# Thirteen layer norms of a transformer stack: column sums by matmul on features-on-partitions against row statistics with tokens turned onto partitions

## The reference

```python
def _layernorm(x, axis=-1, eps=1e-05):
    m = jnp.mean(x, axis=axis, keepdims=True)
    v = jnp.var(x, axis=axis, keepdims=True)
    return (x - m) / jnp.sqrt(v + eps)
...
x = x + _L0_xattn_ref(_layernorm(x), ctx_1024, ctx_1024, ...)
x = x + _L0_ffn_ref(_layernorm(x), ...)          # router, 8 experts of 512
...                                              # layers 1 and 2 alike
x = x + _L3_xattn_ref(_layernorm(x), ctx_1024, ctx_1024, ...)
x = x + _L3_ffn_ref(_layernorm(x), ...)          # router, 9 experts of 256
```

## Time and profile before

| | |
|---|---|
| median of 3 runs | 4042.69 us (4041.46 to 4049.66) |
| the profiled execution | 4052.49 us, its span 4050.8 us |
| PE busy | 3442.2 us, 85% of the span |
| DVE busy | 2414.1 us, 60% |
| ACT busy | 1848.2 us, 46% |
| POOL busy | 1175.3 us, 29% |
| the 13 norms, from first product to last result | 246.89 us, 6.1% of the span |

### The profile page before, as it was taken

The page is one execution under the profiler, slowest core; times in us unless marked ns, Lnnn a source line. Parts: engine busy times, 40 slices in busy tenths (PEclk is TensorE's granted clock), DMA queues, the critical chain, the costliest instruction groups (busy, mean ns, idle before and its releaser), DMA issues. The chain is left out here.

```text
span 4050.8 us, 78638 instructions
## 1 busy us (share of the span) xinstructions
PE 3442.2 (85%) x30966; PEld 2422.0 (60%) x30966; DVE 2414.1 (60%) x4465; ACT 1848.2 (46%) x3390; POOL 1175.3 (29%) x727
## 2 busy tenths in 40 slices
PE   6977986999999999999987998699999973348859
PEld 4643545887778787878865776355555542225534
DVE  2435544776666666767753443688888845646535
ACT  1423323555555555555542543266666631115526
POOL 0002541111111111111112111377777730025507
PEclk6988997999999999999998998699999975569879
DMA  3540002001001000010002664333333300044400
GB/s 72 123 92 33 1 2 67 32 32 47 32 32 45 35 32 32 32 45 35 29 10 89 236 238 174 79 96 85 89 94 83 93 2 6 0 76 92 77 25 10
DMA packets 155773, 253.60 MB, mean 63 GB/s; under 512 B 11301, under 2 KB 114994, under 8 KB 155154
## 3 DMA queue, kind: packets, MB, share of 16 engines
q1 hardware_dynamic: 155410, 248.49, 21.8%
HBM read 173.82 MB, written 74.65 MB: 61 GB/s over the span
## 5 line engine op out<-in xcount | busy, mean ns | idle before, releaser
L1679 DVE TENSOR_SCALAR_CACHE_REDUCE L_p<-L_score,L_cols 128x1500 f32<-128x1500 f32 x224 | 398.7, 1780 | 396.3 <-PE L_score L1515 396.3
L1618 ACT CAST L_pthi<-L_pt 125x512 bf16<-125x512 f32 x672 | 350.5, 593 | 557.1 <-PE L_pt L1524 557.1
L1961 ACT ACTIVATE L2b_p<-L2b_score 125x448 f32<-125x448 f32 x768 | 392.2, 542 | 300.3 <-PE L2b_score L1876 293.9
L1535 PE MATMUL L_acc<-L_chi,L_pthi 125*128 125x128 bf16 x2688 | 462.0, 219 | 0.4 <-DVE L_attn L1699 0.4
L1537 PE MATMUL L_acc<-L_chi,L_ptlo 125*128 125x128 bf16 x2688 | 461.6, 219 | 0.0
L1536 PE MATMUL L_acc<-L_clo,L_pthi 125*128 125x128 bf16 x2688 | 461.5, 219 | 0.0
L1692 DVE TENSOR_TENSOR L_ptlo<-L_pt,L_pthi 125x512 bf16<-125x512 f32 x672 | 418.2, 678 | 1.1 <-ACT L_pthi L1618 1.1
L1602 ACT ACTIVATE L_p<-L_p,L_least 128x1500 f32<-128x1500 f32 x224 | 350.3, 1564 | 7.2 <-DVE L_p L1679 5.2
L1524 PEld LDWEIGHTS L_pt<-ident,L_p 128*125 128x125 f32 x2688 | 332.1, 190 | 33.4 <-issue 1.3
L1524 PE MATMUL L_pt<-ident,L_p 128*125 128x128 f32 x2688 | 333.8, 274 | 0.5 <-ACT L_p L1602 0.4
L2032 DVE TENSOR_REDUCE L2b_max<-L2b_m 112x1 f32<-112x1000 f32 x256 | 301.9, 1193 | 42.0 <-PE L2b_m L1857 41.9
(11 more groups left out here) (595 smaller groups left out, 7219.9 us busy)
## 6 DMA issues: line engine op xcount, KB each, us to landing
L2b_kst<-L_keys SPq DMA_DIRECT2D x96, 375.0 KB, 5.5
L_ctx<-dram_ctx SPq DMA_DIRECT2D x32, 750.0 KB
L_ct<-L_ct SPq DMA_DIRECT2D x32, 750.0 KB
L2a_ct<-L_ct SPq DMA_DIRECT2D x32, 750.0 KB, 14.5
L_keys<-L2a_kout SPq DMA_DIRECT2D x32, 750.0 KB, 7.6
L_values<-L2a_vout SPq DMA_DIRECT2D x32, 750.0 KB
L2b_vin<-L_values SPq DMA_DIRECT2D x32, 750.0 KB
L0x_ctx<-dram_ctx SPq DMA_DIRECT2D x32, 672.0 KB
```

The source lines that it names most:

```text
L1535: pe.matmul(acc, pt_hi[k % 2][:, t, :], c_hi[half][:, t, :], start=(t == 0), stop=False)
L1618: act.copy(pt_hi[k % 2][:, 4 * j:4 * j + 4, :], pt_ps[j][0:KP, :].rearrange("p (t q) -> p t q", t=4)).then_inc(hi_done, 1)
L1679: dve.tensor_scalar(probs[k % 2][:, :].rearrange("p (i n) -> p i n", i=3), score_ps[:, :].rearrange("p (i n) -> p i n", i=3)[:, :, 0:500], ...
L1961: act.activation(probs[t % RP][:, half * 2 * GW:(half + 1) * 2 * GW], score_ps[half][0:KP, 0:2 * GW], ACT.Exp).then_inc(exp_done, 1)
```

## The change

`layernorm` is rewritten for all its calls, and layer 3's L3x_ln and L3x_lnq become one call (`twice`), so there are 12. PE turns the 14 groups of 128 tokens so that tokens stand on partitions (L211). DVE takes the statistics of each group from PSUM with one instruction (L252, it gives count, mean and sum of squares of even and odd elements), and makes variances of five small instructions (L261 to L268), first for groups 0 to 7, then for 8 to 13. POOL's power is in two parts accordingly (L242). ACT scales groups 0 to 7 with a scale and an offset per partition (L226), DVE groups 8 to 13 (L299). PE turns each group back (L217), and ACT copies the first 1024 columns out of PSUM (L234, or L236 with the weight and bias), DVE the rest (L279, or L277). Where the result is added to x, DVE takes all four chunks (L275) and has added the bias to x before (L293). All 8 PSUM banks are used, so that no engine waits for a bank.

```diff
-        layernorm(nc, c, "L3x_ln", c["xT"], c["hT"], 1e-5)
-        layernorm(nc, c, "L3x_lnq", c["hT"], c["hT"], 1e-5, col["w1"][:, :], col["b1"][:, :])
+        layernorm(nc, c, "L3x_lnq", c["xT"], c["hT"], 1e-5, col["w1"][:, :], col["b1"][:, :], twice=True)
...
+    floor = eps * eps / (1.0 + eps) if twice else eps / 4.0 if double else eps
+    grow = 1.0 + eps if twice else 1.0
+    groups = [(0, 4), (4, 4), (8, 4), (12, 2)]
+    halves = [(0, 8), (8, TT)]
...
+            def _(pe):
+                for g, (t0, n) in enumerate(groups):
+                    for t in range(n):
+                        m = pe.transpose(x_ps[g][:, t * 128:(t + 1) * 128], src[:, (t0 + t) * 128:(t0 + t + 1) * 128],
+                                         c["ident"][:, :])
+                    m.then_inc(turned, 1)
+                for g, (t0, n) in enumerate(groups):
+                    pe.wait_ge(first_rows if g < 2 else last_rows, 2 * k + g % 2 + 1)
+                    for t in range(n):
+                        m = pe.transpose(y_ps[g][:, t * 128:(t + 1) * 128], rows[:, t0 + t, :], c["ident"][:, :])
+                    m.then_inc(back_done, 1)
...
+            def _(act):
+                act.wait_ge(offset_ready, 2 * k + 1)
+                for g in (0, 1):
+                    t0, n = groups[g]
+                    for t in range(n):
+                        m = act.activation(rows[:, t0 + t, :], x_ps[g][:, t * 128:(t + 1) * 128], ACT.Identity,
+                                           bias=offset[:, t0 + t:t0 + t + 1], scale=rstd[:, t0 + t:t0 + t + 1])
+                    m.then_inc(first_rows, 1)
+                if add_to is None:
+                    for g in (0, 1):
+                        s, n = cols(g)
+                        act.wait_ge(back_done, 4 * k + g + 1)
+                        if gamma is None:
+                            act.copy(dst[:, s], y_ps[g][:, 0:n])
+                        else:
+                            act.activation(dst[:, s], y_ps[g][:, 0:n], ACT.Identity, bias=beta, scale=gamma)
...
+            def _(pool):
+                for h, (a, b) in enumerate(halves):
+                    pool.wait_ge(var_ready, 2 * k + h + 1)
+                    pool.tensor_tensor(rstd[:, a:b], var[:, a:b], c["half_neg"][:, a:b], ALU.pow).then_inc(rstd_ready, 1)
...
+                def statistics(h):
+                    a, b = halves[h]
+                    for g in (2 * h, 2 * h + 1):
+                        t0, n = groups[g]
+                        dve.wait_ge(turned, 4 * k + g + 1)
+                        for t in range(n):
+                            m = dve.bn_stats(stats[:, t0 + t, :], x_ps[g][:, t * 128:(t + 1) * 128])
+                    m.then_inc(stats_done, 1)
...
+                statistics(0)
+                variance(0)
+                statistics(1)
+                a, b = halves[0]
+                dve.wait_ge(rstd_ready, 2 * k + 1)
+                dve.scalar_tensor_tensor(offset[:, a:b], total[:, a:b], -0.5, rstd[:, a:b], ALU.mult, ALU.mult
+                                         ).then_inc(offset_ready, 1)
+                variance(1)
+                a, b = halves[1]
+                dve.wait_ge(var_ready, 2 * k + 2)
+                dve.tensor_scalar(offset[:, a:b], total[:, a:b], 0.5, None, ALU.mult).then_inc(offset_ready, 1)
+                if add_to is not None:
+                    dve.tensor_scalar(add_to[:, :], add_to[:, :], beta, None, ALU.add).then_inc(added, 1)
...
+                for g in (2, 3):
+                    t0, n = groups[g]
+                    for t in range(n):
+                        m = dve.tensor_scalar(rows[:, t0 + t, :], x_ps[g][:, t * 128:(t + 1) * 128],
+                                              offset[:, t0 + t:t0 + t + 1], rstd[:, t0 + t:t0 + t + 1], ALU.subtract,
+                                              ALU.mult)
+                    m.then_inc(last_rows, 1)
```

More of the change, by code:

```diff
@@ L245, in _ @@
[L245 to L259, removed]
@@ L260, in _ @@
-                for i in range(4):
-                    s, n = cols(i)
-                    dve.wait_ge(r_done, 4 * k + i + 1)
-                    ins = dve.tensor_tensor(dst[:, s], dst[:, s], r_ps[i % 2][:, 0:n], ALU.mult)
-                    ins.then_inc(scaled, 1)
-                    if gamma is not None or add_to is not None:
-                        dve.wait_ge(scaled, 4 * k + i + 1)
-                    if gamma is not None:
-                        st.link(dve.tensor_scalar(dst[:, s], dst[:, s], gamma, beta, ALU.mult, ALU.add))
-                    if add_to is not None:
-                        st.link(dve.tensor_tensor(add_to[:, s], add_to[:, s], dst[:, s], ALU.add))
@@ L271, in _, with variance, part @@
-                c["ln_count"]["steps"] += st.n
+                def statistics(h):
[6 more added lines that the diff above has]
+                    m.then_inc(stats_done, 1)
+                def variance(h):
+                    a, b = halves[h]
+                    def part(i):
+                        return stats[:, a:b, i:i + 1].rearrange("p t o -> p (t o)")
+                    dve.wait_ge(stats_done, 2 * k + h + 1)
+                    dve.tensor_tensor(gap[:, a:b], part(1), part(4), ALU.subtract).then_inc(parts_done, 1)
+                    dve.scalar_tensor_tensor(spread[:, a:b], part(2), D * floor, part(5), ALU.add, ALU.add)
+                    dve.wait_ge(parts_done, 4 * k + 2 * h + 1)
+                    dve.scalar_tensor_tensor(gap[:, a:b], gap[:, a:b], grow / 4.0, gap[:, a:b], ALU.mult, ALU.mult
+                                             ).then_inc(parts_done, 1)
+                    dve.tensor_tensor(total[:, a:b], part(1), part(4), ALU.add)
+                    dve.wait_ge(parts_done, 4 * k + 2 * h + 2)
+                    dve.scalar_tensor_tensor(var[:, a:b], spread[:, a:b], grow / D, gap[:, a:b], ALU.mult, ALU.add
+                                             ).then_inc(var_ready, 1)
@@ new lines, in evacuate @@
+                def evacuate(g):
+                    s, n = cols(g)
+                    dve.wait_ge(back_done, 4 * k + g + 1)
+                    if add_to is not None:
+                        dve.scalar_tensor_tensor(add_to[:, s], y_ps[g][:, 0:n], gamma, add_to[:, s], ALU.mult, ALU.add)
+                    elif gamma is not None:
+                        dve.tensor_scalar(dst[:, s], y_ps[g][:, 0:n], gamma, beta, ALU.mult, ALU.add)
+                    else:
+                        dve.tensor_copy(dst[:, s], y_ps[g][:, 0:n])
@@ new lines, in _ @@
+                if add_to is not None:
+                    dve.tensor_scalar(add_to[:, :], add_to[:, :], beta, None, ALU.add).then_inc(added, 1)
+                dve.wait_ge(offset_ready, 2 * k + 2)
+                dve.wait_ge(rstd_ready, 2 * k + 2)
+                for g in (2, 3):
+                    t0, n = groups[g]
+                    for t in range(n):
[3 more added lines that the diff above has]
+                    m.then_inc(last_rows, 1)
@@ L272, in layernorm @@
+                if add_to is not None:
+                    c["ln_count"]["adds"] += 1
+                    dve.wait_ge(added, c["ln_count"]["adds"])
+                    evacuate(0)
+                    evacuate(1)
+                evacuate(2)
+                evacuate(3)
         c["ln_count"]["calls"] += 1
```

44 lines of the change are left out of this document (16 added, 28 removed).

## The result

The changed kernel takes 3926.60 us, median of 4 runs (3918.55 to 3929.24), against 4042.91 of the kernel before (4041.46 to 4049.66): a ratio of 0.9706, 95% interval 0.9690 to 0.9721, 116.3 us less. A second series gave 3920.0 against 4038.2, ratio 0.9708 (0.9694 to 0.9722); one of its six runs of the changed kernel took 4406.7 us at a granted clock of 0.75, and the ratio, not the median, is without it. Between the two profiled executions the gain is 123.4 us, 24.4 more than forecast, and more than half of that comes from a stretch that the change doesn't touch.

A forecast was written before the change was run, and what follows sets the result against it. Each norm's chain of engines working in turn, with nothing covering it, was taken to bound the kernel. Norms and merge gain 103.9 us, less 5 for the clock: 99, so 4042.7 becomes 3944; range 3928 to 3972 for 8 of 10.

The forecast's parts named there:

- no stretch between norms longer, save the routers' first 4 us: Sign of being right: between norms, only the routers' first 4 us behind a norm would take longer.
- The norms' term: All norms: 12 new ones take 143.3 us in sum, where the 13 old ones took 246.9.
- the chain: One new norm link by link, from first turn to last copy: ACT starts at 5.48, plain norm ends at 11.85 us.
- ACT's eight scalings: In each norm, ACT scales eight groups of 128 columns at 0.39 us each in a row, bounds 0.295 and 0.48.
- the statistics: In each norm, DVE's statistics on 128 columns take 0.20 us in a row, bounds 0.13 and 0.59.
- The clock's charge: Behind norms, routers of layers 0 and 3 start at a lower clock: 5 us charged, between nothing and 8.
- rival 1: After every norm routers and next products start at 1.2 GHz, and turns stay slow: 3951 us; chance 25%.
- The merge: Layer 3's two norms in a row become one: 19.4 us gained by itself, with a meeting of engines of 0.31.
- rival 2: In each norm, DVE's statistics hardly get cheaper with fewer columns, offset 4.7 us later: 4000 us; chance 6%.
- rival 3: In the norms, narrow instructions cost what single wide ones do, a price per instruction: 4050 us; chance 2%.
- rival 4: The merged norm isn't one, or a norm's end is hidden anyway, leaving a fraction of the gain: 3961 us; chance 7%.

The follow-up runs named there:

- N = 8: The kernel before, with 8 idle one-column products more on PE ahead of layer 1's attention loop: 4027.6 us, ratio 0.9969 to the kernel before.
- N = 26: The changed kernel with 26 idle one-column products more on PE ahead of layer 1's attention loop: 3934.2 us (one run).

## Why the prediction was wrong

- **The failed step: a sum with terms for the norms and the clock only.** Every other stretch was put at no change, with nothing to say why ("no stretch between norms longer, save the routers' first 4 us" was a sign of being right, and a shorter one was not thought of). Layer 1's attention lost 13.3 us (13.0 in the mean of two profiles each), since the new norms have fewer PE instructions, and that moved the place of its loop. That an edit can do so was not among my rivals. N = 8 ahead of the loop takes 15 to 16 us out of this stretch in the kernel before, N = 26 puts 15 into the changed one.
- **The norms' term was mis-sized by 6.5 us**: 143.3 forecast, 136.8 measured, 0.4 to 0.9 less for a plain norm. Either this or the loop alone would have left the time inside the range; together they put it 1.4 us below. In L0f_ln, a plain norm at the low clock throughout (start 297.32), the chain is right to 0.05 us up to ACT's start, 5.43 us in, where I had 5.48:

```profile
300.88 1.64 POOL L242 TENSOR_TENSOR L0f_ln_rstd<-L0f_ln_var,half_neg 128x8 f32<-128x8 f32 x1 [41.88 <-DVE L0f_ln_var L268]
302.75 2.90 ACT L226 ACTIVATE L0f_ln_rows<-L0f_ln_x,L0f_ln_offset,L0f_ln_rstd 128x128 f32<-128x128 f32 x8 [33.92 <-DVE L0f_ln_offset L286]
305.71 2.40 PE L217 MATMUL L0f_ln_y<-ident,L0f_ln_rows 128*128 128x128 f32 x10 [0.28 <-ACT L0f_ln_rows L226]
```

ACT's eight scalings are the wrong size: 2.90 us for 3.22, 0.35 each in a row and not 0.39. So PE's last ten turns begin at 8.39 for 8.8 and the norm ends at 11.41 for 11.85. The 0.39 took 0.83 ns a column for the spread of ACT's two rows, which the earlier trace rows don't give: (0.66 - 0.295)/320 is 1.14 ns, and by it the scaling would have come out at 0.295, too low. (In the same way give DVE 1.09 ns a column and not 1.04, which moves the statistics from 0.20 to 0.18; they took 0.21 in a row.) In L1x_ln above the clock rose during the first turns, so the power begins at 3.37 for 3.6 as well.
- **The clock's charge was right**: 4.0 us for 5. Layer 0's router products take 6.11 instead of 3.26, 2.85 more where I had 3.2. Of rival 1 the low clock came true: L0f_ln, L2x_ln2, L2x_ln3, L2f_ln, L3x_lnq and L3f_ln run at 0.50 from end to end. It was in my charge already and cost no 7 us more.
- **The merge** cost one meeting and one norm, as said, though its 19.4 was 16 to 17 by trace in the old form (18.6 by the ratio).
- **Rivals 2, 3 and 4** are out: no price per instruction, no hidden end.
- The sum with measured terms: norms and meeting 110.4, less 4.0, plus 13.3, is 119.7 of the 123.4 us between the two profiled spans. The other 3.7 lie in layers 0 to 3 in pieces of up to 1.2 us. Most are within what a stretch differs by from run to run; the one ahead of L3x_lnq repeats (184.3 and 183.8 us in the two profiles of before, 183.1 and 182.8 after), and its cause is open. The medians' 116.3 is lower because the kernel before was profiled 9.6 above its median and the changed one 2.6 above.

## What to carry to other kernels

When an edit adds or removes many instructions ahead of a hardware loop, look at what PE does at each turn-back of that loop, before and after: a stall on "issue" behind the first products is a matter of place, worth 2 to 3 us a pass here, and a few idle instructions ahead or a loop written out remove it. Where the trace has an instruction only in a wider form, carry both bounds of its length in a row through to the sum: here 0.04 us on one scaling became 0.3 us a norm. Where a timed change and its trace disagree with the sum, list every stretch between the changed ones before explaining the changed ones.

## What the hardware showed that I had not expected

- A turn-back of this hardware loop costs 2.4 to 3.1 us of PE each time even at a good place, with a granted clock of 0.76 in the 7 us behind the first; writing the loop out took 28 us off a stretch with five of them.
- Layer 2's attention from L2x_ln1 to L2x_ln2 has two lengths, 746 to 751 us or 756 to 758, in one and the same kernel (after: 756.8, again 748.7; before: 756.6, again 746.6). That is 8.0 of the 12.1 us between the two profiled spans of the changed kernel and 10.0 of the 16.1 between those of the kernel before. By stretch its last 57 us in the changed kernel, and the last 49 in its second profile:

```profile
3179.14:3235.89 56.75, 50.82 (x515) 26.09 (x513) 30.51 (x42) 29.60 (x61) 35.97 (x18) 0.90 0.01 3
```

```profile
3177.66:3226.40 48.74, 42.81 (x484) 22.42 (x483) 27.14 (x39) 27.37 (x57) 33.21 (x16) 1.00 0.01 2
```

The longer one has a granted clock of 0.90, the shorter 1.00. What makes the clock drop in some executions stays open.
